# Gaps between on-chip buffers, and the last batch's router, norm and store in another order, in a one-core fp32r decoder layer

## The chip, the core and the metric

One NeuronCore of a Trainium2 chip runs the whole kernel. Its engines are TensorE (PE; PEld is its weight load), VectorE (DVE), ScalarE (ACT), GpSimd (POOL) and SyncE (SP), which here only issues DMAs. Each runs its own queue in the order in which the program was written, and they meet at semaphores. The metric is the device time of one launch in microseconds (us). Its operands lie in SBUF, 128 partitions wide. The address of a buffer below is the byte offset inside a partition.

## What is computed

A post-norm decoder layer over 16 batches of 256 tokens and 512 channels: causal attention with 16 query heads and 4 key/value heads, a WKV recurrence against a context, and a dense layer with a 16-expert low-rank adapter that a top-2 router weighs. Each ends in a residual sum and a layer norm.

```python
x = _layernorm(x + attention(x))            # H=16, HKV=4, HD=128, rotary, causal
x = _layernorm(x + wkv(w, u, k=x, v=ctx))   # scan over 256 tokens
# the last third, for every token of x:
h = silu(x @ rw1.T + rb1)
logits = (h @ rw2.T + rb2)[:, :16] + gates
topv, topi = top_k(logits, 2); sm = softmax(topv)
coeff = zeros_like(logits).at[rows, topi].set(sm)
base = x @ W.T + bias
delta = einsum('ner,eor->no', einsum('ni,eri->ner', x, A) * coeff[:, :, None], B)
x = _layernorm(x + base + delta)
```

## The kernel before

**Precision.** Every fp32 operand of a product is split in a high and a low half in the fp32r type (`Xh`, `Xl`, and so on), and `three` (lines 528 to 530) issues three matmuls for each product: high by high, high by low, low by high. Of the 10,500 matmuls in the trace 9,152 are of this kind. The others are transposes against the identity `Ident`, the router's second product (L722) and a warm-up (L738).

**Three stretches.** From slot 0 on, one attention head is taken up in each slot: projection, rotation, scores, softmax, product with V, output product, each some slots behind the other. A tail of the WKV recurrence for one batch runs through the same slots on DVE, ACT and POOL. The weights are staged in through `KVT`, `A2Z`, `E2Z` and `ED` and split on ACT (high) and DVE (low, `splits`, L1431) at slots that the table `SPLIT_AT` gives: the first half's pieces in the order `FIRST_ORDER`, DVE a slot behind ACT. Near the end the third part begins: `step(n, part)` for steps 0 to 19 with three parts each, written out by hand for each engine. The slots' table `PARTS_AT` interleaves the first of them with the last attention work; from about 1,315 us on they stand alone.

**A batch f in the steps.** In step f+1 PE transposes the rows (L667), in step f+2 it makes the low-rank and hidden product (320 columns), turns the hidden values (L713, part 1) and makes the logits (L722, part 2). DVE then picks the two best (L1408 to L1423), POOL makes the coefficients (L1116 to L1120) and weighs the low-rank values into `QB` (L1125). In step f+3 PE turns those (L701), makes the dense product in two halves of the rows (`dense(0)` in bank 5 in part 1, `dense(1)` in bank 6 in part 2, 12 matmuls of 512 columns each) and adds the adapter's product (6 matmuls for each half, `bank<-W,Qh`). In step f+4 DVE has added the residual (L1376), takes mean and variance (`norm_stats`, L1262 to L1267), POOL makes the scale and the shift (L1094 to L1098), ACT applies them (L947) and SP stores the 512 KB (L486). The last batch is f = 15, and `OUT[1]`, its output, lies in `XR`.

**Where the buffers lie.** They are allocated one behind the other. Modulo 128 bytes `W`, `smalls`, `tables` (cosine, sine, mask and identity), `Bo`, `XR`, `Xh`, `Xl`, `KHL`, `Vh`, `Vl`, `QB`, `SW`, `RC`, `KRC`, `Qh`, `Ql` and `S` start at 0; `PTh`, `PTl`, `OTh`, `OTl`, `RO`, `KVT`, `PS` and `ED` at 96, `A2Z` at 32, `E2Z` at 64, `QS` at 0.

Of the kernel before, what the change touches and what calls it, by code (L numbers as in the profile page):

```python
# [68 lines left out]
SPLIT_AT = [[-6, -6, -2, -2, -6, -6, 0, 1, 1, 2, 3, 4] + [h // 2 + 4 for h in range(HEADS)],  # L69
# [106 lines left out]
def decoder(nc, xt, xn, ctxt, wraw, small, bo, wf, wl, wb, fbias, trig_t, late_t, out):  # L176
# [4 lines left out]
    with ctx:  # L181
# [44 lines left out]
        both = lambda table: table[:, :].rearrange("p (a t) -> p a t", a=1).to_broadcast([P, 2, T])  # L226
        Q = [sb(f"Q{i}", [P, 2, T], fr) for i in "hl"]
# [3 lines left out]
        RL = sb("RL", [P, 2, TT])  # L231
        PT = [sb(f"PT{i}", [P, 4, P + T], fr) for i in "hl"]
# [181 lines left out]
        def _(sp):  # L414
# [55 lines left out]
            def step(n, part):  # L470
# [13 lines left out]
                if f is not None and part == 2:  # L484
                    sp.wait_ge(f_done, f + 1)
                    sp.dma_start(out[TAIL_BATCH[f], :, :].rearrange("(a p) c -> p a c", p=P), OUT[f % 2]).then_inc(f_out[f % 2], 16)  # L486
# [35 lines left out]
            for i in range(2):  # L522
                sp.wait_ge(f_out[i], 16 * BATCH // 2)

        @block.tensor
        def _(pe):
# [128 lines left out]
            def step(n, part):  # L655
# [13 lines left out]

                def dense(t):  # L670
# [32 lines left out]
                elif part == 1:  # L703
# [3 lines left out]
                    if f is not None:  # L707
# [6 lines left out]
                        last.then_inc(hid_turned, 1)  # L714
                else:
                    dense(1)
                    turn_x2(1)
                    f = stage_of(n, 2)
                    if f is not None:
                        pe.wait_ge(hid_copied, f + 1)  # L720
                        for a in range(TT):
                            last = nc.tensor.matmul(bank[4][:, T + a * EXP:T + (a + 1) * EXP], HST[:, a * P:(a + 1) * P], Rw2, start=True, stop=True)  # L722
                        last.then_inc(logits_done, 1)
# [18 lines left out]
        def _(act):  # L742
# [161 lines left out]
            def step(n, part):  # L904
# [26 lines left out]
                elif part == 1:  # L931
# [12 lines left out]
                    if f is not None:  # L944
                        act.wait_ge(f_shift, f + 1)
                        for t in range(TT):
                            last = nc.scalar.activation(OUT[f % 2][:, t, :], OUT[f % 2][:, t, :], ACT.Identity,  # L947
                                                        bias=NMF[:, f % 2, t:t + 1], scale=RSF[:, f % 2, t:t + 1])
                        last.then_inc(f_done, 1)
# [30 lines left out]
        def _(pool):  # L980
# [108 lines left out]
            def step(n, part):  # L1089
                f = stage_of(n, 4)  # L1090
                if f is not None and part == 0:
                    pool.wait_ge(f_ve, f + 1)
                    above(pool, f_done, f - 1)
                    gp.tensor_tensor(RSF[:, f % 2, :], VEF[:, f % 2, :], Mhalf[:, :], ALU.pow).then_inc(f_rs, 1)  # L1094
                    pool.wait_ge(f_rs, f + 1)
                    gp.tensor_tensor(NMF[:, f % 2, :], MVF[:, f % 2, :, 0], RSF[:, f % 2, :], ALU.mult).then_inc(f_rs2, 1)
                    pool.wait_ge(f_rs2, f + 1)
                    gp.tensor_scalar(NMF[:, f % 2, :], NMF[:, f % 2, :], -1.0, None, ALU.mult).then_inc(f_shift, 1)  # L1098
# [35 lines left out]
        def _(dve):  # L1134
# [125 lines left out]
            def norm_stats(tiles, par, stats, mv, ve, done):  # L1260
                for t in range(TT):
                    v.bn_stats(stats[:, par, t, :], tiles[:, t, :])  # L1262
                dve.drain()
                for t in range(TT):
                    v.bn_aggr(mv[:, par, t, :], stats[:, par, t, :])
                dve.drain()
                v.tensor_scalar(ve[:, par, :], mv[:, par, :, 1], EPS, None, ALU.add).then_inc(done, 1)  # L1267
# [93 lines left out]
            def step(n, part):  # L1361
# [16 lines left out]
                if part == 0:  # L1378
                    out_sum(4, 1)
                    f = stage_of(n, 4)  # L1380
                    if f is not None:
                        dve.wait_ge(f_sum, TT * f + TT)
                        above(dve, f_shift, f - 1)
                        norm_stats(OUT[f % 2], f % 2, STF, MVF, VEF, f_ve)
# [16 lines left out]
                else:  # L1401
# [24 lines left out]
                    out_sum(3, 0)  # L1426

# [74 lines left out]
```

## Time and profile before

| | us |
|---|---|
| median of 3 runs | 1603.1 |
| lowest, highest | 1602.74, 1606.97 |
| profiled execution, time | 1607.82 |
| profiled execution, span in the trace | 1606.0 |
| busy: PE / PEld / DVE / ACT / POOL | 1556.0 / 1413.4 / 1340.3 / 1115.5 / 1007.7 |
| mean granted TensorE clock, share of full speed | 0.991 |

The page's busy time of PE is the time in which at least one matmul is under way. Matmuls overlap, so the pace of a stream of them is read from the starts of neighbours in the timeline, not from the mean duration. The span is from the first to the last instruction; the profiled execution's time is 1.8 us longer.

### The profile page before, as it was taken

To read this page: it belongs to the slowest core of one execution; us is meant where nothing else is said; L and a number is where in the kernel's file an instruction comes from. 1 tells how busy PE (TensorE), PEld (TensorE's weight loads), DVE (VectorE), ACT (ScalarE), POOL (GpSimd) and SP (SyncE) were. 2 spreads that over 40 slices of the span, in tenths; PEclk is the share of its full clock that TensorE was granted. 3 is DMA by queue.
4 is the path that set the end of the run, shared out by engine and by line. 5 is a ranking of instruction groups with operands and counts; after the bars stand their busy time and mean duration, and the time that the engine had idled before them with its cause. 6 is when DMAs were issued, how large, how long until landed. Compare 5 with 4: busy or idle time off the path is not lost.

```text
span 1606.0 us, 32704 instructions
## 1 busy us (share of the span) xinstructions
PE 1556.0 (97%) x10500; PEld 1413.4 (88%) x10500; DVE 1340.3 (83%) x3434; ACT 1115.5 (69%) x2995; POOL 1007.7 (63%) x850
## 2 busy tenths in 40 slices
PE   8999999999999999999999999999999987989997
PEld 7899999999999999999999999999999976878785
DVE  6776688889888889898999889898989897877863
ACT  6777787877787778777877787878787865334332
POOL 2665586757675867676767666676667653635653
PEclk9999999999999999999999999999999999999999
DMA  9765344324442444244424442445144522121211
GB/s 298 256 225 201 112 150 137 116 73 142 150 137 55 152 146 136 60 152 151 139 60 152 151 139 60 132 146 164 44 126 148 178 70 79 53 93 66 80 66 53
DMA packets 81625, 202.62 MB, mean 126 GB/s; under 512 B 10416, under 2 KB 11056, under 8 KB 81456
## 3 DMA queue, kind: packets, MB, share of 16 engines
q1 hardware_dynamic: 81456, 200.53, 40.0%
q8 instruction: 86, 1.41, 0.4%
q14 instruction: 83, 0.68, 0.1%
HBM read 120.80 MB, written 37.75 MB: 99 GB/s over the span
## 4 chain that ended last, share of the span: by engine, by line
PE 84%; DVE 7%; issue 3%; POOL 2%; ACT 1%; DVEq 1%; DMA 1%; SPq 0%; ACTq 0%; POOLq 0%
PE bank L528 25%; PE bank L529 24%; PE bank L530 24%; PE bank L652 5%; PE bank L597 2%; PE bank L643 1%; PE bank L598 1%; PE bank L635 1%; DVE PS L1328 1%; DVE ED L1339 1%; PE bank L667 1%; DMA SW<-QB 1%; DVE SW L1392 0%; DVE RC L1170 0%; DVE OTl L1243 0%
## 5 line engine op out<-in xcount | busy, mean ns | idle before, releaser
L528 PE MATMUL bank<-Xh,W 128*128 128x256 f32 x1280 | 362.2, 283 | 5.8 <-DVE RC L1170 2.5
L529 PE MATMUL bank<-Xl,W 128*128 128x256 f32 x1280 | 360.5, 282 | 0.0
L530 PE MATMUL bank<-Xh,W 128*128 128x256 f32 x1280 | 360.4, 282 | 0.0
L1025 POOL TENSOR_TENSOR Ql<-RC,Qh 128x512 fp32r<-128x512 f32 x127 | 169.6, 1336 | 208.9 <-ACT Qh L744 208.7
L759 ACT ACTIVATE S<-S,NM 128x128 f32<-128x128 f32 (+1 forms) x512 | 228.2, 447 | 65.8 <-DVE NM L1155 65.2
L528 PEld LDWEIGHTS bank<-Xh,W 128*128 128x128 f32 x1280 | 241.3, 189 | 9.2 <-DVE RC L1170 5.1
L1013 POOL TENSOR_TENSOR SW<-SW,tables 128x512 f32<-128x512 f32 x128 | 170.8, 1334 | 124.6 <-DMA SW<-QB 124.5
L744 ACT ACTIVATE PTh<-bank 128x384 fp32r<-128x384 f32 x256 | 124.9, 488 | 173.1 <-PE bank L652 173.1
L529 PEld LDWEIGHTS bank<-Xl,W 128*128 128x128 f32 x1280 | 241.7, 189 | 0.0
L530 PEld LDWEIGHTS bank<-Xh,W 128*128 128x128 f32 x1280 | 241.6, 189 | 0.0
L744 ACT ACTIVATE S<-S,RL 128x128 f32<-128x128 f32 (+1 forms) x512 | 203.4, 448 | 31.7 <-DVE RL L1162 31.5
L528 PE MATMUL bank<-W,OTh 128*128 128x512 f32 x512 | 203.2, 397 | 4.9 <-DVE RO L1254 3.3
L529 PE MATMUL bank<-W,OTh 128*128 128x512 f32 x512 | 203.6, 398 | 0.0
L530 PE MATMUL bank<-W,OTl 128*128 128x512 f32 x512 | 203.1, 397 | 0.0
L1017 POOL TENSOR_TENSOR RC<-RC,SW 128x512 f32<-128x512 f32 x127 | 177.9, 1401 | 18.2
L528 PE MATMUL bank<-W,Xh 128*128 128x256 f32 (+2 forms) x512 | 166.4, 325 | 1.5 <-DVE RC L1170 1.4
L529 PE MATMUL bank<-W,Xh 128*128 128x256 f32 (+2 forms) x512 | 163.2, 319 | 0.0
L530 PE MATMUL bank<-W,Xl 128*128 128x256 f32 (+2 forms) x512 | 163.0, 318 | 0.0
L1170 DVE SCALAR_TENSOR_TENSOR RC<-bank,smalls,tables 128x256 f32<-128x256 f32 x256 | 119.6, 467 | 44.0 <-ACT QB L777 43.7
L1141 DVE TENSOR_TENSOR PTl<-bank,PTh 128x384 fp32r<-128x384 f32 x256 | 140.9, 550 | 2.2 <-ACT PTh L744 1.9
L1151 DVE TENSOR_TENSOR S<-bank,tables 128x128 f32<-128x128 f32 x256 | 72.5, 283 | 80.2 <-PE bank L530 79.7
L652 PE MATMUL bank<-tables,S 128*128 128x128 f32 x768 | 126.4, 273 | 1.5 <-DVE PTl L1141 1.4
(161 smaller groups left out, 4450.1 us busy)
## 6 DMA issues: line engine op xcount, KB each, us to landing
W<-kept SPq DMA_DIRECT2D x140, 512.0 KB, 4.5
SW<-QB SPq DMA_DIRECT2D x256, 128.0 KB, 2.3
kept<-W SPq DMA_DIRECT2D x40, 512.0 KB, 5.0
XR<-XR SPq DMA_DIRECT2D x64, 128.0 KB, 2.3
RO<-in_xn SPq DMA_DIRECT2D x16, 512.0 KB, 4.1
KVT<-in_ctxt SPq DMA_DIRECT2D x16, 512.0 KB, 4.2
mixed<-RO SPq DMA_DIRECT2D x16, 512.0 KB, 3.8
XR<-in_xt SPq DMA_DIRECT2D x15, 512.0 KB, 4.2
```

The costliest lines, as they stand in the source:

```text
L528: nc.tensor.matmul(dst, lhs[0], rhs[0], start=first, stop=False)
L529: nc.tensor.matmul(dst, lhs[0], rhs[1], start=False, stop=False)
L530: return nc.tensor.matmul(dst, lhs[1], rhs[0], start=False, stop=last)
L652: last = nc.tensor.transpose(pt_ps[:, k * P:(k + 1) * P], S[:, g % 2, k * P:(k + 1) * P], Ident[:, :])
L744: return nc.scalar.activation(dst, src, ACT.Copy, **kw)
L759: last = nc.scalar.activation(S[:, i, c], S[:, i, c], ACT.Exp, bias=NM[:, i, t:t + 1], scale=-1.0, accum_out=L[:, i, t:t + 1])
L1013: gp.tensor_tensor(SW[:, :, :], SW[:, :, :], both(Sin), ALU.mult).then_inc(q_sin, 1)
L1017: gp.tensor_tensor(RC[:, i % 2, :, :], RC[:, i % 2, :, :], SW[:, :, :], ALU.add).then_inc(q_summed, 1)
L1025: gp.tensor_tensor(Q[1][:, :, :], RC[:, i % 2, :, :], Q[0][:, :, :], ALU.subtract).then_inc(q_lo, 1)
L1141: v.tensor_tensor(PT[1][:, g % 4, :], pt_ps[:, 0:P + T], PT[0][:, g % 4, :], ALU.subtract).then_inc(pt_lo, 1)
L1151: v.tensor_tensor(S[:, i, 0:P], s_ps[:, P:T], Mask[:, 0:P], ALU.add).then_inc(masked, 1)
L1170: v.scalar_tensor_tensor(out=RC[:, g // 2 % 2, g % 2, :], in0=proj_ps("Q", g, 0), scalar=Bq[:, SEQ[g // HEADS][0], h:h + 1], in1=Cos[:, :] ...
```

## The change

It has five parts. (1) Four buffers named gap0 to gap3 that nothing reads or writes, 64, 64, 64 and 32 bytes wide, are allocated in front of `Xh`, of `KHL`, of `Qh` and of `PTh`. Modulo 128 `Xh`, `Xl`, `Qh`, `Ql`, `S`, `PTh`, `PTl`, `OTh`, `OTl`, `RO`, `KVT`, `PS` and `ED` then start at 64, `A2Z` and `QS` at 0 and 96, `E2Z` at 32, and the others stay at 0. (2) The weight piece of the first half's fifth query head is split a slot later, together with the sixth's. (3) For the last batch PE makes the logits right behind the turned hidden values, in part 1 of step 17, ahead of `dense(1)` of batch 14. (4) For the last batch DVE takes the statistics of the first 128 rows before it adds the residual of the second 128, and POOL and ACT work on each half by itself. (5) The last batch is stored in two DMAs of 256 KB.

```diff
-SPLIT_AT = [[-6, -6, -2, -2, -6, -6, 0, 1, 1, 2, 3, 4] + [h // 2 + 4 for h in range(HEADS)],
+SPLIT_AT = [[-6, -6, -2, -2, -6, -6, 0, 1, 2, 2, 3, 4] + [h // 2 + 4 for h in range(HEADS)],
...
+        def gap(i, n):
+            sb(f"gap{i}", [P, n // 4])
         XR = sb("XR", [P, KC, T])
+        gap(0, 64)
         X = [sb(f"X{i}", [P, 2, KC, T], fr) for i in "hl"]
+        gap(1, 64)
         KHL = sb("KHL", [P, 2, JL, 2, T], fr)
...
+        gap(2, 64)
         Q = [sb(f"Q{i}", [P, 2, T], fr) for i in "hl"]
         S = sb("S", [P, 2, P + T])
...
+        gap(3, 32)
         PT = [sb(f"PT{i}", [P, 4, P + T], fr) for i in "hl"]
...
-                    sp.wait_ge(f_done, f + 1)
-                    sp.dma_start(out[TAIL_BATCH[f], :, :].rearrange("(a p) c -> p a c", p=P), OUT[f % 2]).then_inc(f_out[f % 2], 16)
+                    rows = out[TAIL_BATCH[f], :, :].rearrange("(a p) c -> p a c", p=P)
+                    if f < LAST:
+                        sp.wait_ge(f_done, f + 1)
+                        sp.dma_start(rows, OUT[f % 2]).then_inc(f_out[f % 2], 16)
+                    else:
+                        for t in range(TT):
+                            sp.wait_ge(f_done, f + t + 1)
+                            sp.dma_start(rows[:, t, :], OUT[f % 2][:, t, :]).then_inc(f_out[f % 2], 16)
...
+                def logits():
+                    f = stage_of(n, 2)
+                    if f is not None:
+                        pe.wait_ge(hid_copied, f + 1)
+                        for a in range(TT):
+                            last = nc.tensor.matmul(bank[4][:, T + a * EXP:T + (a + 1) * EXP], HST[:, a * P:(a + 1) * P], Rw2, start=True, stop=True)
+                        last.then_inc(logits_done, 1)
...
                         last.then_inc(hid_turned, 1)
+                        if f == LAST:
+                            logits()
                 else:
                     dense(1)
                     turn_x2(1)
-                    f = stage_of(n, 2)
-                    if f is not None:
...
+                    if stage_of(n, 2) != LAST:
+                        logits()
...
-                        act.wait_ge(f_shift, f + 1)
                         for t in range(TT):
+                            act.wait_ge(f_shift, f + 1 + t * (f == LAST))
                             last = nc.scalar.activation(OUT[f % 2][:, t, :], OUT[f % 2][:, t, :], ACT.Identity,
                                                         bias=NMF[:, f % 2, t:t + 1], scale=RSF[:, f % 2, t:t + 1])
-                        last.then_inc(f_done, 1)
+                            if f == LAST or t == TT - 1:
+                                last.then_inc(f_done, 1)
...
+                    for k, those in enumerate((slice(0, 1), slice(1, 2)) if f == LAST else (slice(0, TT),)):
+                        pool.wait_ge(f_ve, f + k + 1)
+                        gp.tensor_tensor(RSF[:, f % 2, those], VEF[:, f % 2, those], Mhalf[:, those], ALU.pow).then_inc(f_rs, 1)
...
-                        norm_stats(OUT[f % 2], f % 2, STF, MVF, VEF, f_ve)
+                        norm_stats(OUT[f % 2], f % 2, STF, MVF, VEF, f_ve, range(f == LAST, TT))
...
                     out_sum(3, 0)
+                    if stage_of(n, 3) == LAST:
+                        dve.wait_ge(f_sum, TT * LAST + 1)
+                        dve.wait_ge(f_shift, LAST - 1)
+                        norm_stats(OUT[LAST % 2], LAST % 2, STF, MVF, VEF, f_ve, range(1))
```

Line numbers of the changed kernel are some lines higher: L528 to L530 become L546 to L548, L713 becomes L739, L722 L693, L1376 L1403, L1431 L1462.

**PE, step 17**, where the logits of the last batch stand. Before:

```order
L530 MATMUL bank5<-W,Xl 128x512
L713 MATMUL bank4<-tables,SW 64x128 x2
L528 MATMUL bank6<-W,Xh 128x512
L529 MATMUL bank6<-W,Xh 128x512
...
L530 MATMUL bank6<-W,Xl 128x512
L722 MATMUL bank4<-smalls,SW 128x16 x2
L528 MATMUL bank5<-W,Qh 128x512
```

And in the changed kernel:

```order
L548 MATMUL bank5<-W,Xl 128x512
L739 MATMUL bank4<-tables,SW 64x128 x2
L693 MATMUL bank4<-smalls,SW 128x16 x2
L546 MATMUL bank6<-W,Xh 128x512
L547 MATMUL bank6<-W,Xh 128x512
...
L548 MATMUL bank6<-W,Xl 128x512
L546 MATMUL bank5<-W,Qh 128x512
```

The two logits matmuls have moved past the 12 matmuls of `dense(1)` of batch 14.

**DVE, the last rows of the program**, behind the low half of the last adapter operand (`Ql`). Before:

```order
L1398 TENSOR_TENSOR Ql<-bank1,Qh 128x512
L1376 TENSOR_TENSOR XR<-bank5,KRC 128x512
L1376 TENSOR_TENSOR XR<-bank6,S 128x512
L1262 BN_STATS STF<-XR 128x6 x2
L1265 BN_AGGR MVF<-STF 128x2 x2
L1267 TENSOR_SCALAR VEF<-MVF 128x2
```

And in the changed kernel:

```order
L1425 TENSOR_TENSOR Ql<-bank1,Qh 128x512
L1403 TENSOR_TENSOR XR<-bank5,KRC 128x512
L1288 BN_STATS STF<-XR 128x6
L1291 BN_AGGR MVF<-STF 128x2
L1294 TENSOR_SCALAR VEF<-MVF 128x1
L1403 TENSOR_TENSOR XR<-bank6,S 128x512
L1288 BN_STATS STF<-XR 128x6
L1291 BN_AGGR MVF<-STF 128x2
L1294 TENSOR_SCALAR VEF<-MVF 128x1
```

The first half's statistics now stand between the two residual sums.

**DVE, slots 2 to 4 at the start**, the low halves of the weight pieces (`W<-E2Z,W`, `W<-ED,W`) among the first heads' work. Before:

```order
L1431 TENSOR_TENSOR W<-E2Z,W 128x512
L1431 TENSOR_TENSOR W<-ED,W 128x512
L1170 SCALAR_TENSOR_TENSOR RC<-bank0,smalls,tables 128x256
L1216 TENSOR_TENSOR Vl<-bank1,Vh 128x256
L1202 TENSOR_TENSOR KHL<-KRC,KHL 128x2x256
L1183 TENSOR_TENSOR RC<-RC,SW 128x512
L1186 TENSOR_TENSOR Ql<-RC,Qh 128x512
L1431 TENSOR_TENSOR W<-ED,W 128x512
L1170 SCALAR_TENSOR_TENSOR RC<-bank1,smalls,tables 128x256
```

And in the changed kernel:

```order
L1462 TENSOR_TENSOR W<-E2Z,W 128x512
L1196 SCALAR_TENSOR_TENSOR RC<-bank0,smalls,tables 128x256
L1242 TENSOR_TENSOR Vl<-bank1,Vh 128x256
L1228 TENSOR_TENSOR KHL<-KRC,KHL 128x2x256
L1209 TENSOR_TENSOR RC<-RC,SW 128x512
L1212 TENSOR_TENSOR Ql<-RC,Qh 128x512
L1462 TENSOR_TENSOR W<-ED,W 128x512 x2
L1196 SCALAR_TENSOR_TENSOR RC<-bank1,smalls,tables 128x256
```

One low half has moved behind the first heads' `Ql`; its high half on ACT has moved in the same way, from ahead of the third head's `QB` to just ahead of the `KHL` copy.

## Rows read from the trace of the kernel before

**Rows 1.** Busy time by stretch: start:end, its length, PE's busy time, granted clock, DMA share, GB/s

```profile
100.00:1290.00 1190.00, 1188.65 (x8384) 1.00 0.42 130
...
1354.00:1364.00 10.00, 7.20 (x38) 1.00 0.16 52
...
1481.00:1491.00 10.00, 8.25 (x44) 1.00 0.01 2
...
1587.00:1592.00 5.00, 5.00 (x19) 0.66 0.26 100
```

**Rows 2.** Timeline of PE: start, duration, what; ends of three even runs of matmuls

```profile
502.59 0.39 PE L528 MATMUL bank<-W,OTh 128*128 128x512 f32 x1
...
503.75 0.40 PE L530 MATMUL bank<-W,OTl 128*128 128x512 f32 x1
...
505.73 0.29 PE L528 MATMUL bank<-Xh,W 128*128 128x256 f32 x1
...
508.10 0.28 PE L530 MATMUL bank<-Xh,W 128*128 128x256 f32 x1
...
1594.30 0.40 PE L528 MATMUL bank<-W,Qh 128*128 128x512 f32 x1
...
1596.86 0.40 PE L530 MATMUL bank<-W,Ql 128*128 128x512 f32 x1
```

**Rows 3.** Groups of PE instructions by line: transposes, busy us, mean ns, idle before

```profile
L643 PE MATMUL bank<-tables,E2Z 128*128 128x128 f32 x128 | 19.8, 278 | 3.7 <-DVE RO L1350 3.7
L635 PE MATMUL bank<-tables,RO 128*128 128x128 f32 x128 | 19.5, 275 | 3.0 <-DVE RO L1350 1.6 <-ACT KVT L744 1.4
```

**Rows 4.** Two lines' POOL instructions: count, duration ns min/median/max, first and last start

```profile
L1062 POOL TENSOR_TENSOR E2Z<-PS,KVT x32: 1085/1287/1539, 234.4 to 1504.9; 128x512 f32<-128x512 f32 x32
...
L1025 POOL TENSOR_TENSOR Ql<-RC,Qh x127: 1267/1292/2222, 31.8 to 1314.6; 128x512 fp32r<-128x512 f32 x127
```

**Rows 5.** Timeline of all engines, steps 17 and 18: the last batch's router

```profile
1578.04 0.38 ACT L744 ACTIVATE SW<-bank 64x256 f32<-64x256 f32 x1 [1.53 <-PE bank L713]
...
1580.71 0.61 PE L722 MATMUL bank<-smalls,SW 64*128 64x16 f32 x4
...
1581.36 0.19 DVE L1408 TENSOR_TENSOR S<-bank,smalls 128x32 f32<-128x32 f32 x1 [3.71 <-PE bank L722]
...
1583.91 0.40 PE L530 MATMUL bank<-W,Ql 128*128 128x512 f32 x1
...
1586.68 0.66 PE L701 MATMUL bank<-tables,QB 128*128 128x128 f32 x4 [2.38 <-POOL QB L1125]
...
1587.10 0.48 PE L528 MATMUL bank<-W,Xh 128*128 128x512 f32 x1
```

**Rows 6.** Timeline of all engines, the last batch's residual, norm and store

```profile
1597.29 0.69 DVE L1376 TENSOR_TENSOR XR<-bank,S 128x512 f32<-128x512 f32 x1 [0.71 <-PE bank L530]
1598.02 1.29 DVE L1262 BATCH_NORM_STATS2 STF<-XR 128x6 f32<-128x512 f32 x2
...
1599.95 0.71 POOL L1094 TENSOR_TENSOR RSF<-VEF,Mhalf 128x2 f32<-128x2 f32 x1 [11.62 <-DVE VEF L1267]
...
1601.29 1.52 ACT L947 ACTIVATE XR<-XR,NMF,RSF 128x512 f32<-128x512 f32 x2 [11.41 <-POOL NMF L1098]
1602.84 0.37 SPq L486 DMA_DIRECT2D out_x<-XR  x1
```

**Rows 7.** DMA issues by line: count, KB each, median us to landing

```profile
out_x<-XR SPq DMA_DIRECT2D x2, 512.0 KB, 2.7
...
SW<-QB SPq DMA_DIRECT2D x256, 128.0 KB, 2.3
```

**Rows 8.** Timeline of the start, slots 2 to 5

```profile
23.12 0.69 DVE L1431 TENSOR_TENSOR W<-ED,W 128x512 fp32r<-128x512 f32 x1
...
28.42 0.47 ACT L777 ACTIVATE QB<-bank,smalls 128x256 f32<-128x256 f32 x1 [2.05 <-DMA SW<-QB]
...
29.46 0.39 PE L528 MATMUL bank<-Xh,W 128*128 128x256 f32 x1 [1.43 <-DVE RC L1170]
```

More of the change, by code:

```diff
@@ L406, in run @@
                     step(n, part)
+        LAST = BATCH - 1
         def stage_of(n, lag):
@@ L522, in _ @@
             for i in range(2):
-                sp.wait_ge(f_out[i], 16 * BATCH // 2)
+                sp.wait_ge(f_out[i], 16 * (BATCH // 2 + (i == LAST % 2)))
         @block.tensor
@@ L717, in step @@
                     turn_x2(1)
-                    f = stage_of(n, 2)
-                    if f is not None:
[L720 to L723, printed above, removed]
+                    if stage_of(n, 2) != LAST:
+                        logits()
                     f = stage_of(n, 3)
@@ L1091, in step @@
                 if f is not None and part == 0:
-                    pool.wait_ge(f_ve, f + 1)
                     above(pool, f_done, f - 1)
[L1094 to L1098, printed above, removed]
+                    for k, those in enumerate((slice(0, 1), slice(1, 2)) if f == LAST else (slice(0, TT),)):
+                        pool.wait_ge(f_ve, f + k + 1)
+                        gp.tensor_tensor(RSF[:, f % 2, those], VEF[:, f % 2, those], Mhalf[:, those], ALU.pow).then_inc(f_rs, 1)
+                        pool.wait_ge(f_rs, f + k + 1)
+                        gp.tensor_tensor(NMF[:, f % 2, those], MVF[:, f % 2, those, 0], RSF[:, f % 2, those], ALU.mult).then_inc(f_rs2, 1)
+                        pool.wait_ge(f_rs2, f + k + 1)
+                        gp.tensor_scalar(NMF[:, f % 2, those], NMF[:, f % 2, those], -1.0, None, ALU.mult).then_inc(f_shift, 1)
                 f = stage_of(n, 2)
@@ L1258, in odd, with norm_stats @@
                 tail(n, 0)
-            def norm_stats(tiles, par, stats, mv, ve, done):
-                for t in range(TT):
+            def norm_stats(tiles, par, stats, mv, ve, done, which=range(TT)):
+                for t in which:
                     v.bn_stats(stats[:, par, t, :], tiles[:, t, :])
                 dve.drain()
-                for t in range(TT):
+                for t in which:
                     v.bn_aggr(mv[:, par, t, :], stats[:, par, t, :])
                 dve.drain()
-                v.tensor_scalar(ve[:, par, :], mv[:, par, :, 1], EPS, None, ALU.add).then_inc(done, 1)
+                those = slice(which.start, which.stop)
+                v.tensor_scalar(ve[:, par, those], mv[:, par, those, 1], EPS, None, ALU.add).then_inc(done, 1)
             def norm_shift(par, mv, rs, nm):
```

## Prediction

> **What bounds the kernel now.** I read the busy time by stretch first. From 100 to 1,290 us PE is busy for 1,188.65 of 1,190 us at a granted clock of 1.00, the higher of the two levels, 2.4 GHz [rows 1]. In that stretch nothing but the pace of PE's own stream counts: what is gained on DVE, ACT or POOL comes to nothing there. So the change has two places where it can act: the pace of the matmuls, which the gaps might touch, and the ends of the program, where PE waits and where the last batch's norm and store hang behind it.
>
> **The gaps, PE.** After them the moving and the stationary operand of nearly all products lie 64 bytes apart modulo 128 (`Xh` 64 and `W` 0, `Qh` 64 and `KHL` 0, `PTh` 64 and `Vh` 0, `OTh` 64 and `W` 0). Before, they are 0 apart (`Xh`/`W`, `Qh`/`W`) or 32 apart (`OTh`/`W`). The timeline gives the paces [rows 2]: 20 matmuls of 256 columns, 0 apart, from 505.73 to 508.10, 118.5 ns each; 5 of 512 columns, 32 apart, from 502.59 to 503.75, 232.0 ns; 11 of 512 columns, 0 apart, from 1594.30 to 1596.86, 232.7 ns. So 0 or 32 apart makes 0.7 ns of 232, or 0.3%. The nearest to 64 are the transposes of `E2Z`, whose blocks lie 68 to 80 bytes from the identity's: 278 ns in the mean beside 275 ns for those of `RO`, 32 apart [rows 3]. No row has an fp32r pair 64 apart. I take 0 for it, since neither the one step shown nor the nearest neighbour moves the pace. The bounds are 0.3% of the 1,189 us either way, 3.6 us, and a rival below takes what lies beyond.
>
> The trace has both of PE's streams, moving data and the next weights, under way at once at this pace, whatever lies where. The Trainium skill (SBUF — State Buffer, Who interferes with whom) gives PE two independent read ports and says that PE and ACT never wait on anyone; by that rule this term is exactly 0, and no row here contradicts it, but none is at 64. The same notes (TensorE: Matmul & The Clock Gate, Back-to-back issue gap) give N/2.4 + 2.5 ns for isolated matmuls, 109.2 and 215.8 ns for 256 and 512 columns. If the rest of the 118.5 and 232.7 ns were a conflict that the gaps end, an estimate by that page over some 6,000 and 2,500 matmuls would be 56 + 42 = 98 us off, about 1,500 us. I do not use it in the sum.
>
> **The gaps, POOL and DVE.** The duration of a GpSimd sum does depend on something of this kind: the same line L1062 takes 1,085 ns at least and 1,287 ns in the median, and its two halves differ in nothing but their addresses (`PS` 0 or 8 bytes past `KVT` modulo 128) [rows 4]. `Ql<-RC,Qh`, now 0 apart and then 64, takes 1,292 ns in the median [rows 4]. 127 of those, anything from 26 us of POOL's time off to as much on, all of it beside a PE that does not wait [rows 1]. Worth 0; that cover is gone only where PE waits for `Ql` in the first 50 us, three waits, so 0.2 us each: 0.6 us either way.
>
> **The logits ahead of `dense(1)`.** Now PE turns the hidden values, ACT copies them from 1578.04 to 1578.42, and PE comes to the logits only at 1580.71, behind 12 matmuls. DVE begins at 1581.36, and POOL's `QB` lets PE go on at 1586.68, after 2.38 us of idleness; PE's last matmul before that started at 1583.91 [rows 5]. In the new order PE waits for ACT's copy: logits at 1578.50 instead of 1580.71, so DVE, and all that follows on DVE, ACT and POOL, 2.2 us earlier, and `QB` lets PE go at 1584.5. ACT has its norm of batch 13 between the copy and the router's exponential, 1.5 us by the like of it [rows 6], over at about 1579.8, when the exponential's input is due. What is queued behind the new wait on PE is `dense(1)` and the adapter of batch 14: 12 matmuls that started behind the turn now start behind the logits, PE idles about 0.5 us, and its last matmul starts at about 1584.5 instead of 1583.91. DVE's residual of batch 14 waits for that, 0.6 us later, and the last batch's `dense` products, which need the bank, do not: they start later still. Now both PE and `QB` are due at 1584.5, so PE turns `QB` at about 1584.75, **1.9 us earlier**. What is late next is PE itself.
>
> **The clock.** PE's granted clock reads 0.66 from 1587 to 1592, a stretch in which PE never stops, right after the 2.38 us of idleness [rows 1, 5]. The 24 matmuls of both `dense` halves took 1587.10 to 1594.30, 7.20 us, where 24 at 232.7 ns are 5.58: **1.6 us** lost. Around 1481 to 1491 PE is idle for 1.75 us in sum and the clock stays at 1.00 [rows 1]. With 0.5 us of idleness left I expect no fall. Against it: from 1354 to 1364, with 2.8 us idle, it did not fall either [rows 1], so whether it falls is not settled by the gap alone, and the runs near the median may not all have had it.
>
> **The norm and the store by halves.** Take PE's last matmul start, 1596.86, as T [rows 2]. Now the second residual starts at T + 0.43, both statistics at T + 1.16, POOL at T + 3.09, ACT at T + 4.43, the store at T + 5.98, and the span ends 3.16 us later [rows 6]. The first half's residual stands 6 matmuls earlier, at T - 0.97, done at T - 0.28. Its statistics take 1.93 us less one of the two passes and one aggregation, about 1.2 us, so DVE is free at T + 0.95: the second residual is 0.5 us late, and the second statistics, shorter by 0.7, are done at T + 2.9, about 0.15 us earlier than now. POOL does the first half's three steps meanwhile (1.34 us). So ACT scales the second half at T + 4.3 for half of 1.52 us, and the last store is issued at T + 5.1 instead of T + 5.98: 0.9 us. The store then carries 256 KB. By the rows a 512 KB store lands after 2.7 us and a 128 KB copy after 2.3 [rows 7]; the last one's 3.16 us less 0.2 to 0.9, I take 0.5. The other half has landed by then. **1.4 us** in sum. The Trainium skill (SBUF — State Buffer, The DMA setup-cost knee) has about 2 us fixed and the bytes at 436 GB/s behind them: 0.6 us less for half the bytes, so 1.5 us by that page.
>
> **The start.** DVE has 0.69 us [rows 8] of splitting less before the first `Ql` and as much more behind it; on ACT one high half, 0.53 us, slips ahead of the `KHL` copy. Ahead of it nothing is won: the work that follows waited for PE. Behind it `Ql` is 0.5 us and the next head's `RC` 1.1 us later. PE's next wait, 1.43 us at 29.46, ends with `RC`, which waits for `QB`, which waits 2.05 us for a DMA [rows 8]. If that DMA is held up by its backlog, the delay is swallowed; if it starts 0.5 us later, all behind it is 0.5 us later. **0.3 us** lost, between 0 and 1.1.
>
> **The sum.** 1.9 + 1.6 + 1.4 - 0.3 = 4.6 us, with 0 for the gaps. Against the profiled execution, 1607.8 - 4.6 = 1603.2. That execution is 4.7 us slower than the median, and I do not know which waits or clock falls make this; I take the same 4.6 us off the median: **1598.5 us**. Without the clock term it is 1600.1; with PE's pace 0.3% better 1594.9, and 0.3% worse 1602.1.
>
> **Rivals.**
> *The gaps speed up the fp32r matmuls.* For it: the pace above the columns alone. From 256 to 512 columns it grows by 114.2 ns, so some part is not columns; POOL's line shows that addresses can matter on this chip. Against it: 0 and 32 apart are alike. Each ns is 9.2 us on 9,152 matmuls: 1 ns gives 1589.3, 5 ns 1552.5.
> *The gaps slow them down.* Same place, the other sign: if 64 apart costs, the 4.6 us are eaten at 0.5 ns for each of the 9,152, and at 1 ns the kernel stands at 1607.7, slower than before. Against it: the same two paces.
> *The ends give back less.* The clock falls anyway, at another place, and the start costs 1.1 us: 4.6 - 1.6 - 0.8 = 2.2, so 1600.9. For it: the fast runs, of which I have no trace.
>
> **Chances.** Forecast 0.55, own range 1594.9 to 1602.1; gaps faster 0.20; gaps slower 0.07; less at the ends 0.18. A measurement of this kernel tells 0.3%, 4.8 us, from no change: the bound is 1598.3 and the forecast lies on it. So half of its 0.55 goes to faster, with 0.20 from the gaps: 0.48. Same has the other half and 0.18: 0.45. Slower 0.07. The range takes the forecast's and the lesser gain, and of the faster gaps the part up to 1 ns: 1589 to 1603.
>
> **What would show it.** Right: matmul starts 118.5 and 232 ns apart as before; the last batch's logits 0.5 us behind the turn of its hidden values; PE idle under 0.7 us ahead of the last turn of `QB`; granted clock 1.00 behind it; two stores, the last issued 5.1 us behind PE's last start. Wrong: another pace in the middle stretch, where 1 ns outweighs all the rest twice over; a clock fall in the last 20 us; a first PE wait beyond 50 us.

## The result, and the profile after

| us | before | after | ratio (95%) |
|---|---|---|---|
| median, 4 runs each, beside one another | 1604.7 (1602.7 to 1607.0) | 1588.5 (1586.0 to 1590.6) | 0.9898 (0.9875 to 0.9921) |
| profiled execution: time, span | 1607.8, 1606.0 | 1587.5, 1585.7 | |

Faster by 16 us, 1.0%. The forecast was 1598.5, its range 1589 to 1603: the time lies half a microsecond below the range. In a later round (`after_again`, below) the changed kernel had 1588.8 beside 1608.5, ratio 0.9876 (0.9861 to 0.9891).

The busy time by stretch, which answers to [rows 1] (start:end, length, PE's busy time, granted clock, DMA share, GB/s):

```profile
100.00:1290.00 1190.00, 1180.79 (x8449) 1.00 0.42 130
...
1570.00:1575.00 5.00, 5.00 (x26) 1.00 0.01 3
```

PE starts 65 matmuls more in the same 1,190 us (8,449 beside 8,384) although it is busy for 7.9 us less. The two lines of each pair below are the first and the last start of an even run, at the place of [rows 2]: 24 projections of 256 columns and 6 output products of 512 in the changed kernel.

```profile
500.33 0.28 PE L546 MATMUL bank<-Xh,W 128*128 128x256 f32 x1
...
502.96 0.28 PE L548 MATMUL bank<-Xh,W 128*128 128x256 f32 x1
503.07 0.39 PE L546 MATMUL bank<-W,OTh 128*128 128x512 f32 x1
...
504.22 0.40 PE L548 MATMUL bank<-W,OTl 128*128 128x512 f32 x1
```

23 steps in 2.63 us are 114.3 ns each, where [rows 2] have 118.5; 5 steps in 1.15 us are 230 ns, where they have 232. And PE now waits in the middle. Waits of PE between 60 and 1,290 us (what waits, for what, us in total, times, longest), where the kernel before has one line, `RC`, 0.6 us in 2:

```profile
PE bank L546 <- DVE RC L1196: 5.9, 13, 0.8
PE bank L661 <- DVE RO L1377: 1.6, 4, 0.5
PE bank L546 <- DVE OTl L1269: 1.4, 1, 1.4
PE bank L615 <- POOL Ql L1050: 0.2, 1, 0.2
```

Since both kernels issue the same 10,500 matmuls in nearly the same order, the starts can be subtracted one by one. A step between neighbours is counted as a wait where in either kernel it is over 90 ns longer than usual for its width, and as pace otherwise (us):

| up to matmul | start before | start after | earlier by | pace | waits |
|---|---|---|---|---|---|
| 9,000 | 1287.3 | 1274.5 | 12.75 | +20.3 | -7.5 |
| 10,000 | 1495.5 | 1481.9 | 13.6 | +21.1 | -7.5 |
| the last | 1596.9 | 1578.4 | 18.5 | +22.1 | -3.6 |
| span's end | 1606.0 | 1585.7 | 20.3 | | |

So up to matmul 10,000 PE's pace gave 21.1 us and new waits took 7.5 back; behind it the end gave 4.9, and what follows PE's last start 1.9. The 20.3 are 14.3 from `Xh` and `Xl` moving, 4 from output products (`OTh`), 1.1 from `PTl`. A second trace of the same kernel (`after_again`) has the same pace by matmul 9,000, +20.6, but waits of -9.9: the waits differ by 2 us between executions, the pace hardly.

The end, timeline of all engines, answers to [rows 5, 6]:

```profile
1563.26 0.38 ACT L768 ACTIVATE SW<-bank 64x256 f32<-64x256 f32 x1 [1.49 <-PE bank L739]
1563.69 0.61 PE L693 MATMUL bank<-smalls,SW 64*128 64x16 f32 x4 [0.47 <-ACT SW L768]
...
1569.67 0.39 PE L548 MATMUL bank<-W,Ql 128*128 128x512 f32 x1
...
1569.90 0.60 PE L727 MATMUL bank<-tables,QB 128*128 128x128 f32 x4
...
1578.40 0.40 PE L548 MATMUL bank<-W,Ql 128*128 128x512 f32 x1
...
1579.19 0.15 DVE L1294 TENSOR_SCALAR VEF<-MVF 128x1 f32<-128x1 f32 x1
1579.26 0.68 DVE L1403 TENSOR_TENSOR XR<-bank,S 128x512 f32<-128x512 f32 x1
...
1580.69 0.81 ACT L971 ACTIVATE XR<-XR,NMF,RSF 128x512 f32<-128x512 f32 x1 [4.98 <-POOL NMF L1124]
...
1581.53 2.08 SPq L504 DMA_DIRECT2D out_x<-XR  x2
...
1582.43 0.81 ACT L971 ACTIVATE XR<-XR,NMF,RSF 128x512 f32<-128x512 f32 x1 [0.93 <-POOL NMF L1124]
```

PE waits 0.47 us for the hidden values and not at all for `QB`; the store goes out in two halves.

### The profile page after: what moved, and what is told of

Read it like the earlier page. It is cut to its first block, busy times and chain, and to the rows that moved or that the text cites. A ratio compares the mean times of both kernels' runs of the same rounds, so it can differ in the third digit from the quotient of the medians.

```text
span 1585.7 us, 32712 instructions
## 1 busy us (share of the span) xinstructions
PE 1533.6 (97%) x10500; PEld 1395.1 (88%) x10500; DVE 1337.7 (84%) x3435; ACT 1114.7 (70%) x2995; POOL 1007.2 (64%) x853
## 4 chain that ended last, share of the span: by engine, by line
PE 68%; DVE 14%; issue 6%; ACT 5%; POOL 5%; DMA 1%; DVEq 1%; SPq 0%; ACTq 0%; POOLq 0%
PE bank L546 20%; PE bank L548 20%; PE bank L547 19%; PE bank L670 4%; DVE PS L1325 2%; PE bank L615 1%; DMA SW<-QB 1%; DVE PS L1355 1%; DVE RC L1196 1%; PE bank L653 1%; PE bank L661 1%; ACT Xh L768 1%; DVE PTl L1167 1%; DVE OTl L1269 1%; POOL SW L1038 1%
## 5 line engine op out<-in xcount | busy, mean ns | idle before, releaser
L546 PE MATMUL bank<-Xh,W 128*128 128x256 f32 x1280 | 357.5, 279 | 8.1 <-DVE RC L1196 5.5
L548 PE MATMUL bank<-Xh,W 128*128 128x256 f32 x1280 | 356.0, 278 | 0.0
L547 PE MATMUL bank<-Xl,W 128*128 128x256 f32 x1280 | 355.7, 278 | 0.0
L1050 POOL TENSOR_TENSOR Ql<-RC,Qh 128x512 fp32r<-128x512 f32 x127 | 170.4, 1342 | 195.8 <-ACT Qh L768 195.5
L783 ACT ACTIVATE S<-S,NM 128x128 f32<-128x128 f32 (+1 forms) x512 | 228.2, 448 | 67.9 <-DVE NM L1181 67.5
L546 PEld LDWEIGHTS bank<-Xh,W 128*128 128x128 f32 x1280 | 241.4, 189 | 11.3 <-DVE RC L1196 6.6
L548 PEld LDWEIGHTS bank<-Xh,W 128*128 128x128 f32 x1280 | 241.0, 188 | 0.0
L546 PE MATMUL bank<-W,OTh 128*128 128x512 f32 x512 | 201.5, 394 | 5.0 <-DVE RO L1280 3.3
L548 PE MATMUL bank<-W,OTl 128*128 128x512 f32 x512 | 203.0, 396 | 0.0
L546 PE MATMUL bank<-W,Xh 128*128 128x256 f32 (+2 forms) x512 | 165.5, 323 | 2.9 <-DVE RC L1196 2.9
L548 PE MATMUL bank<-W,Xl 128*128 128x256 f32 (+2 forms) x512 | 161.5, 315 | 0.0
```

The source lines that it names most:

```text
L546: nc.tensor.matmul(dst, lhs[0], rhs[0], start=first, stop=False)
L547: nc.tensor.matmul(dst, lhs[0], rhs[1], start=False, stop=False)
L548: return nc.tensor.matmul(dst, lhs[1], rhs[0], start=False, stop=last)
L783: last = nc.scalar.activation(S[:, i, c], S[:, i, c], ACT.Exp, bias=NM[:, i, t:t + 1], scale=-1.0, accum_out=L[:, i, t:t + 1])
L1050: gp.tensor_tensor(Q[1][:, :, :], RC[:, i % 2, :, :], Q[0][:, :, :], ALU.subtract).then_inc(q_lo, 1)
```

## The experiments

**1. The parts apart.** `gaps_only` is before with the four gaps, `ends_only` the changed kernel without them and with the old slot in `SPLIT_AT`.

> The kernel before with the four gaps and nothing else. Theory A (an fp32r matmul starts sooner behind its neighbour when moving and stationary operand lie 64 bytes apart modulo 128): 11 to 15 us off, ratio 0.991 to 0.993, about 13.6 us less at the last matmul, since the trace of the changed kernel gains 13.6 us by its 10,000th matmul, ahead of the edits at the end; Xh and W products of 256 columns start 114.9 ns apart instead of 118.7. Rival B (the ends, or the split moved by a slot, made most of the gain): within 4 us of before, ratio 0.998 to 1.002.

> The changed kernel without the gaps and with the old slot for the fifth query head's weight piece: only the last batch's logits, norm and store are changed. Theory A: 4.9 us off as predicted, between 4 and 7, ratio 0.9955 to 0.9975. Rival B: 12 us or more off.

| | median | before beside it | ratio (95%) | pace, waits to matmul 9,000 |
|---|---|---|---|---|
| `gaps_only` | 1593.8 | 1609.0 | 0.9909 (0.9896 to 0.9923) | +20.2, -8.2 |
| `ends_only` | 1602.8 | 1609.0 | 0.9958 (0.9944 to 0.9972) | none |

The gaps alone give 15 us and the ends 6. Their sum, 21 us, is more than the 16 of the result and near the 19.7 of `after_again`. Rival B is out.

**2. Distance or place.** `all_shifted` has one gap of 64 bytes in front of `W`; nothing moves against anything else.

```diff
+        gap(9, 64)
         W = sb("W", [P, NP, 2, PW], fr)
```

> The kernel before with one 64-byte gap ahead of W, so that W and every buffer behind it move by 64 bytes and no two of them move against each other. Theory A (it is the distance between the two operands): no change, ratio 0.998 to 1.002, 118.7 ns as before. Rival C (it is where a moving operand itself lies, 64 instead of 0): as much as the gaps alone, ratio 0.991 to 0.993.

1606.8 beside 1609.0, ratio 0.9989 (0.9980 to 0.9999); the pace to matmul 9,000 differs by 0.25 us. The same 24 projections:

```profile
505.51 0.28 PE L532 MATMUL bank<-Xh,W 128*128 128x256 f32 x1
...
508.23 0.28 PE L534 MATMUL bank<-Xh,W 128*128 128x256 f32 x1
```

118.3 ns, as before. So it is how the buffers lie against one another, not where they all lie. The medians of the 12 steps of a query projection, over 191 groups, are 119 118 118 117 120 119 115 117 122 120 119 118 ns in both; in the changed kernel they are 114 and 113. Medians over all groups hide two kinds there: right behind the product with V (`PTh` by `Vh`) all 112 groups free of waits run at 113 ns from their first step on (1,360 ns for 12), but those behind the scores (`KHL`) begin, in the median, with 118 121 116 115 ns and fall to 114 only then.

**3. PE alone, first program.** 60 matmuls in a row, one buffer for each distance.

> Another program: 60 matmuls in a row on 128 partitions with nothing between them, for each distance of the moving operand (Ma 0 bytes modulo 128, Mb 16, and so on to Mh 112) from the stationary one (Sa 0, Se 64), for 256 and 512 columns of fp32r, twice over; then 128 columns of fp32r and of fp32 (F) at 0 and 64. It computes nothing of the reference. Theory A: for 256 columns about 118.7 ns apart at distance 0 and 114.9 at 64, for 512 columns 232.5 and 229, and Se with Me (both at 64) as Sa with Ma. Rival C: Se with Me as Sa with Me. Rival D (the pace depends on the other engines' traffic, not on PE's own two reads): all distances alike.

Paces behind the first ten matmuls, from the second sweep (the first agrees to 0.1 ns but for its first stream, at a lower clock, and one of 512): at 0, 16, 32, 48, 64, 80, 96, 112 bytes, 256 columns 120.0, 118.7, 116.7, 119.2, 117.8, 119.2, 120.0, 117.1 and 512 columns 226.7, 233.3, 233.3, 233.3, 228.9, 230.0, 233.3, 236.7 ns; 128 columns 111.7 throughout. `Se` with `Me` is 118.7 and 232.4, neither as `Sa` with `Ma` nor as `Sa` with `Me`. So addresses matter with no other engine at work, against rival D, but neither theory A nor rival C had the values.

**4. Which gap.** `x_only` has the first two gaps, `rest_only` the last two.

> The kernel before with the gaps ahead of Xh and of KHL only: X moves by 64 bytes, all behind it by 128. Theory A: 3.9 ns on 3,520 projections with X moving, 2.1 on 960 with W moving and some ns on 352 of 512 columns make 16 to 17 us of pace; with the new waits on DVE 8 to 13 us less, ratio 0.992 to 0.995.

> The kernel before with the gaps ahead of Qh and of PTh only: Q, PT, OT and all behind them move, X and W stay. Theory A: 3.5 ns on 1,536 output products is 5.4 us, less 9 ns on 192 and more 2 ns on 512 of the probabilities' about even: 3 to 7 us off, ratio 0.9955 to 0.998. If the gaps ahead of X make all of the gain: ratio 0.999 to 1.001.

`x_only`: 1596.4 beside 1606.2, 0.9941 (0.9927 to 0.9955), pace +12.2, waits -4.3. `rest_only`: 1604.6, 0.9991 (0.9983 to 1.0000), pace +0.7, waits -0.4: less than expected. Together they make 20.3, so 7.4 us belong to neither. The steps show where. Of the 112 query projections behind the product with V, 67 run at 117 to 118 ns to their end with `X` alone (1,412 ns for 12) and 45 take 1,387; before, all take about 1,417, with all gaps 1,360. Behind the scores they begin, in the median, with 121 122 116 115 ns and then fall to 114. `Xh` lies as far from `W` in both kernels, so this distance is not all that counts. That the matmuls ahead, whose operands the other gaps move, leave something behind fits these steps; it is not shown apart from them.

**5. PE alone, the kernel's patterns.** Groups of `three`, the kernel's strides, one operand read from 0 to 112 bytes on.

> Another program, computing nothing of the reference: PE alone, with the kernel's own groups of three matmuls, their accumulation and their strides, on buffers that all begin at 0 modulo 128, and one operand read from 0, 16, 32 ... 112 bytes behind its buffer's start. Seven patterns, 56 streams of 60 to 96 matmuls: query projection (X moving 256), value projection (W moving 256), output (OT stationary, W moving 512), dense (X stationary, W moving 512), low (the same with 320), scores, probabilities by V. The uniform streams before gave 120.0 and 117.8 ns at distance 0 and 64 for 256 columns but 226.7 and 228.9 for 512, so the distance alone does not order the paces. Theory A (PE's two reads by themselves, in the kernel's pattern): query projection 118.7 ns at 0 and 114.9 at 64, value projection 118.3 and 116.3, output 232 at 96 and 229 at 64, each within 0.5 ns of what the kernels' traces show. Rival D (the other engines' traffic is needed): the same two streams differ by less than 1 ns, or as in the uniform streams.

Query projections 117.8 ns at all distances but 96 (118.6); value projections 119.2 at 0 and 113.3 at 64; output and dense products, with the same addresses, agree within 0.3 ns and go from 230.0 (48) to 235.6 (16). Theory A missed all three patterns: 117.8 ns for 114.9 in the query projections at 64; 119.2 and 113.3 for 118.3 and 116.3 in the value projections, the right sign at three times the size; 233.3 (96) and 231.9 (64) for 232 and 229 in the output products.

> Another program, computing nothing of the reference, PE alone. Query projections by themselves were 117.8 ns apart whatever the distance, while value projections went from 119.2 at 0 to 113.3 at 64, and in the changed kernel both are seen. Theory E (the pace of a matmul depends on the addresses and on what state the stream before it left): 60 query projections at distance 64 run at 113 to 114 ns behind 12 value projections and at 117.8 behind an idle engine; at distance 0 they stay at 118 to 120 behind either. Then 8 slots of one position in the kernel's own order (scores, probabilities by V, projections, output, transposes), 286 matmuls with nothing of the other engines, in 11 sets of distances (X, Q, PT, OT, S). Theory A in this wider form: before's set to the changed kernel's set, the slots get 60 to 70 ns for each projection of 12 shorter, as in the kernels (1421 to 1360 ns), about 2% in sum, x_only between them, rest_only within 0.3% of before. Rival D (other engines' traffic is needed): the four sets within 0.3%.

It had 280 matmuls for each set. Query projections at 64 behind value projections: 117.1 ns, not 113. The four sets took 39.61, 39.58, 39.49 and 39.61 us. Theory E and the wider theory A failed, and D seemed to hold. What I had overlooked: the buffers of these programs lay other than the kernel's modulo 256. In the kernel `Xh` minus `W` was 128 before and is 192 now; in these programs, at "64" modulo 128 `Xh` in my query stream was at 64 modulo 256, and `W` minus `Xh` in my value stream at 192; `Xl` lay another 128 bytes off, since `Xh` was 8,320 bytes long.

**6. Modulo 256.** Buffers all alike modulo 2,048, 16 offsets, and the 8 slots in the kernels' own distances.

> Another program, computing nothing of the reference, PE alone. The slots of the last one did not show the kernels' difference (1405 to 1420 ns for 12 projections in both sets), but its buffers lay other than the kernels' modulo 256. Theory F (the distance that counts is moving minus stationary address modulo 256, and 192 is the fast one): before 128, the changed kernel 192 for Xh against W; value projections in the small programs at 64 were W minus X = 192, and fast; query projections there at 64, and not. So 60 query projections at 192 take 113.3 ns each and 117 to 119 elsewhere, value projections 113.3 at 64 and slower elsewhere, and 192 + 256, + 512 and + 1,024 are as 192. The 8 slots in the kernels' own distances modulo 2,048: 12 projections 1,421 ns by before's and 1,360 by the changed kernel's, 1.5 to 2% in sum. If Theory F is wrong the two sets differ by less than 0.3%, as in the last program, and the other engines' traffic is needed (Rival D).

Windows over single streams: query projections at 128 and 192, value projections with `X` at 64 and 192; query projections at 704 and 448; then the 8 slots by before, the changed kernel, `x_only`, `rest_only`:

```profile
101.90:109.40 7.50, 7.32 (x60) 1.00 0.01 2
132.50:139.90 7.40, 7.09 (x60) 1.00 0.00 0
193.30:200.80 7.50, 7.09 (x60) 1.00 0.00 0
254.40:262.00 7.60, 7.34 (x60) 1.00 0.01 2
757.10:764.70 7.60, 7.33 (x60) 1.00 0.00 0
749.80:757.20 7.40, 7.09 (x60) 1.00 0.01 2
803.10:843.50 40.40, 40.07 (x280) 1.00 0.01 1
843.50:883.20 39.70, 39.40 (x280) 1.00 0.00 1
883.20:923.00 39.80, 39.62 (x280) 1.00 0.00 1
923.00:963.30 40.30, 40.02 (x280) 1.00 0.00 1
```

7.09 us are 113.3 ns a matmul once the stream runs, 7.3 are 117.8 to 118.7. Query projections are fast at 192 (and at 112), value projections with `X` at 64, which is `W` minus `X` at 192. The slots are 1.7% (by the changed kernel's distances), 1.1% (`x_only`) and 0.1% (`rest_only`) shorter than by before's; the kernels' pace to matmul 9,000 is 20.3, 12.2 and 0.7 us better of 1,287: 1.6, 0.9 and 0.1%. PE's own reads suffice for a difference of this size, and rival D is out. Not all of theory F holds: 448 is fast, but 704 and 1,216, also 192 modulo 256, ran at 117.8 ns from an idle engine.

The same in the kernel: `other_64` has `gap(0, 192)` and `gap(1, 192)`, so `Xh` minus `W` is 64 modulo 256.

> The changed kernel with the first two gaps 192 bytes wide instead of 64: Xh still lies 64 bytes from W modulo 128, but at 64 instead of 192 modulo 256, and everything behind KHL stays where it was modulo 256. Theory A as first stated (modulo 128): as the changed kernel, ratio 0.988 to 0.991. Theory F (modulo 256): query projections about 117.8 ns apart instead of 114.8, 3 ns on 3,520, 10 us, value projections 3 ns less on 960, 3 us back: ratio 0.993 to 0.995.

```profile
502.43 0.28 PE L546 MATMUL bank<-Xh,W 128*128 128x256 f32 x1
...
505.15 0.28 PE L548 MATMUL bank<-Xh,W 128*128 128x256 f32 x1
```

118.3 ns. Behind the product with V all query projections are at 117 to 118 ns a step (1,413 for 12). Value projections are of two kinds, nearly in turn: 29 groups at 113 to 114 ns and 29 at 118. The single stream had 113.3 for this distance only; and the changed kernel has 21 of 56 at 113 and `x_only` 30 of 57 at `W` minus `X` = 64, where the stream had 117.8. So for value projections the distance modulo 256 does not tell the pace. 1593.1 beside 1608.7, 0.9907 (0.9894 to 0.9921): pace +11.4, waits -4.1, so 8.9 us of pace are lost against the changed kernel, of which 3.4 come back as waits that go too; the ratio lies between the forecasts of theories A and F. Everything behind `KHL` has also moved by 256 bytes here, which theory F takes for nothing.

**7. What limits next.** DVE's two scans stand ahead of the rotation `RC` for which PE waits. Timeline of DVE in the changed kernel:

```profile
461.25 1.74 DVE L1348 TENSOR_TENSOR_SCAN QS<-A2Z,E2Z 128x514 f32<-128x514 f32 x1
462.92 2.24 DVE L1355 TENSOR_TENSOR_SCAN PS<-A2Z,E2Z 128x514 f32<-128x514 f32 x1
465.08 0.13 DVE L1188 RECIPROCAL RL<-L 128x2 f32<-128x2 f32 x1
465.14 0.46 DVE L1196 SCALAR_TENSOR_TENSOR RC<-bank,smalls,tables 128x256 f32<-128x256 f32 x1
```

```diff
-PS_AT = [(10, 1), (12, 0)]
+PS_AT = [(11, 0), (12, 0)]
```

> The changed kernel with one DVE scan (PS, first half, 2.2 us) a slot later, so that it does not stand right behind the scan of QS in front of the rotation RC for which PE now waits 0.3 to 0.9 us in 13 slots (5.9 us in sum). If these waits cost what they show: 3 to 6 us less than the changed kernel, ratio to before 0.986 to 0.988. Rival (DVE's work is only moved, and PE waits a slot later): as the changed kernel, 0.990.

1593.1 beside 1606.8, 0.9913 (0.9897 to 0.9929): no gain, as the rival has it. PE now waits 8.1 us for `RC` in 17 places.

> The changed kernel with DVE's four scans of each recurrence (QS 1.74 us, PS 2.24 us) replaced by plain sums of the same operands, some 0.6 us each: DVE has about 5.5 us less in each of 16 tails, and the second third of the layer is not computed rightly. Theory G (behind the faster PE, DVE is the next bound, and the new waits are its): PE's waits between 60 and 1,290 us fall from 12.6 us to under 5, and the time is 6 to 10 us less than the changed kernel's, ratio to before 0.984 to 0.986. Rival (the waits come from elsewhere): ratio as the changed kernel's, 0.989.

> The kernel before with the same cheap scans, again not the reference's second third. Theory G: PE waited only 3.2 us in the middle stretch, so at most that comes back, 0 to 3 us, ratio 0.998 to 1.000, against 6 to 10 us in the changed kernel. Rival: as much as there.

In both kernels the cheap sums leave out the recurrence. The cut for `PS`; `QS` has the same:

```diff
-v.tensor_tensor_scan(in_row(PS, h), in_row(A2Z, h), in_row(E2Z, h), 0.0, ALU.mult, ALU.add).then_inc(ps_done, 1)
+v.tensor_tensor(in_row(PS, h), in_row(A2Z, h), in_row(E2Z, h), ALU.add).then_inc(ps_done, 1)
```

1576.9 and 1599.8 beside 1608.5: 0.9797 (0.9783 to 0.9810) and 0.9945 (0.9931 to 0.9959). PE's waits in the changed kernel, with cheap scans:

```profile
PE bank L661 <- DVE RO L1377: 2.0, 5, 0.5
...
PE bank L546 <- DVE RC L1196: 0.5, 2, 0.3
```

The waits for `RC` are gone but for 0.5 us, and 11.9 us in all beside the changed kernel's 1588.8, more than either expectation. But before gains 8.7 too, against my expectation: 2.7 by matmul 9,000 and most of the rest behind it. By matmul 9,000 the cheap scans give 6.6 us beside the changed kernel's first trace and 8.6 beside its second, so 3.9 to 5.9 of them are owed to the faster PE (3 by the medians of the whole). The cheap scans take away more than the order of DVE's work, so the last pair changes only the order.

```diff
+                if tail_of(n, 11) is None:
                     cosines(n)
...
                         if h == 0:
+                            cosines(n + 1)
                             dve.wait_ge(z_done, 2 * tau + 2)
```

> The changed kernel with DVE's rotation RC of the next head put between the two scans QS and PS (1.7 and 2.2 us) instead of behind both, in the 32 slots where they stand together; nothing is left out and no load changes. PE waits 5.9 us in 13 places for just this RC. Theory G: those waits go, PE's waits between 60 and 1,290 us fall from 12.6 to about 7 us, ratio to before 0.984 to 0.987 where the changed kernel has 0.988 to 0.990. Rival (PE catches up with another DVE result a few instructions on, as with the scan put later): 0.988 to 0.991.

**1582.8** beside 1607.2, 0.9847 (0.9833 to 0.9860). The changed kernel had 0.9898 and 0.9876, so this is 5 to 8 us faster, and the intervals do not touch. Pace +20.9, waits -2.4 instead of -7.5 and -9.9. DVE:

```profile
460.45 1.74 DVE L1349 TENSOR_TENSOR_SCAN QS<-A2Z,E2Z 128x514 f32<-128x514 f32 x1
462.12 0.45 DVE L1196 SCALAR_TENSOR_TENSOR RC<-bank,smalls,tables 128x256 f32<-128x256 f32 x1
462.49 1.87 DVE L1357 TENSOR_TENSOR_SCAN PS<-A2Z,E2Z 128x514 f32<-128x514 f32 x1
```

**8. Can the small program choose distances?** `gap(2, 192)` and `gap(3, 160)`, in the changed kernel and with the rotation first.

> The changed kernel with the third gap 192 bytes wide instead of 64 and the fourth 160 instead of 32: Q and S 128 bytes further, at 192 instead of 64 from W modulo 256, all behind PT at 256 further and so the same modulo 256. In the program of PE alone 8 slots took 38.93 us with this distance and 39.13 with the changed kernel's, 0.20 us over 32 positions: 6.4 us less pace. Theory F with G: PE's pace 5 to 7 us better by the starts, of which DVE lets through a part, 2 to 5 us, ratio to before 0.986 to 0.989. If the small program does not foretell a kernel: 0.989 or more.

> The same with the third gap 192 and the fourth 160 bytes wide. Its pace in the trace was 2.3 us worse than the changed kernel's by the 9,000th matmul and its waits 1.5 us less, so the same as the run before it within 2 us: ratio 0.984 to 0.988.

`q_further`: 1588.2, 0.9876 (0.9860 to 0.9891), as the changed kernel beside it; its pace is 2.3 us worse, not 6.4 better. `rotation_first_q`: 1585.3, 0.9866 (0.9851 to 0.9881). Of the 113 query projections behind the product with V in `q_further`, 54 now take about 1,413 ns, where all took 1,360. But this was not a clean trial of the small program. Its set for `q_further` left `PT` and `OT` at 448 and the transposed rows at 1,344 modulo 2,048, and in the kernel `PT` and `OT` lie at 704 and `S` at 1,472. That 256 bytes more can change a pace, the single streams had shown: 448 is fast and 704 is not. Whether the small program gets 0.5% right with the kernel's true distances was not tried.

**9. The start and the measure.**

> The changed kernel with the fifth query head's weight piece split in its old slot. By my step the start is 0.3 us better, between 0 and 1.1; the traces of the first 80 us say the move gained about 1 us, so up to 1 us slower. Ratio to before 0.989 to 0.991 either way.

> The changed kernel itself, beside the other three on their chip: ratio 0.988 to 0.992 as measured before.

`after_old_start`: 1588.4 beside 1606.8, 0.9886 (0.9871 to 0.9901): no difference that can be told.

## Why the prediction was wrong, step by step

**The gaps, PE: 0 with bounds of 3.6 us. This step failed.** Measured 20 to 22 us of pace. Three things were wrong in it. The bounds came from "neither the one step shown nor the nearest neighbour moves the pace": one difference between two distances, taken for a flat curve, where the small program (`micro_256`) has 113.3 to 120.0 ns between 16 offsets. The neighbour was no neighbour: transposes of 128 columns take 109 ns a step in every trace, their mean durations 278 and 276 now beside 278 and 275 [rows 3]; nor does the stream of 128 fp32r columns move. And distances were taken modulo 128, where the streams at 0 and 128 bytes (120.0 and 118.7 ns), and at 64 and 192 (117.8 and 113.3), differ. The mean of 118.5 ns hid a pattern of 115 to 122 that a look at single steps in the trace of before would have shown.

By the rule of the Trainium skill (SBUF — State Buffer, Who interferes with whom), two independent read ports for PE, which never waits on anyone, this term would be exactly 0. The small programs, with PE alone, do not bear it out for PE's own two reads: 7.09 or 7.3 us for the same 60 matmuls, by their addresses.

**Rival: the gaps speed up fp32r matmuls**, chance 0.20, was right in its mechanism: addresses set part of the pace above the columns. The 22 us are 2.4 ns in the mean by its 9.2 us per ns; the range took only the first ns.

**"What is gained on DVE ... comes to nothing there" [rows 1]** was not quite so for before, and wrong behind a faster PE. With cheap scans before gains 3.1 us between 100 and 1,287 us, mostly in eleven places where a projection starts 0.18 to 0.45 us sooner, though the view of its waits shows only 0.6 us. With DVE's order changed behind the faster PE 5.7 to 7.8 us come out of the same stretch. The rival lacked this too: 7.5 to 9.9 of its 20 us went into waits, most of them for `RC`.

**The gaps, POOL and DVE: 0.** Right. POOL is busy for 1007.2 us (1007.7 before), and `Ql<-RC,Qh` means 1,342 ns (1,336), though its operands moved by 64:

```profile
L1050 POOL TENSOR_TENSOR Ql<-RC,Qh 128x512 fp32r<-128x512 f32 x127 | 170.4, 1342 | 195.8 <-ACT Qh L768 195.5
```

**The logits, 1.9 us.** Right. PE waits 0.47 us for them (0.5 said), and PE itself is what is late next. Matmuls 10,120 to 10,460 hold both the old wait for `QB` and the new one for the logits: 67.5 to 67.9 us in the six kernels with the old end, 65.5 to 65.9 in the ten traces with the new one: 2.1 us.

**The clock, 1.6 us.** The size is right, the occurrence is not certain. The last 39 matmuls take 10.2 us in before and in `gaps_only` and 10.0 in `before_cheap_scans`, 8.5 to 8.6 in those ten, but also in `all_shifted`, `x_only` and `rest_only`, which have the old end. Windows around PE's last wait, in before, `gaps_only` and `all_shifted`:

```profile
1584.90:1590.90 6.00, 4.22 (x15) 0.75 0.03 9
```

```profile
1568.80:1574.80 6.00, 4.12 (x13) 0.72 0.01 3
```

```profile
1582.50:1588.50 6.00, 3.62 (x18) 1.00 0.01 3
```

So behind the same wait the clock fell in some executions and not in others: "Whether it falls is not settled by the gap alone" was right, and the median of before probably holds only a part of the 1.6 us. The same executions differ by another 1.1 us that I had not seen: between matmul 10,000 and 10,120 before and `gaps_only` take 23.46 us and the others 22.3 to 22.4 (the late scan 23.1, `before_cheap_scans` 23.0). In before PE waits 1.08 us there for `QB`, in the changed kernel 0.21:

```profile
1498.72 0.66 PE L727 MATMUL bank<-tables,QB 128*128 128x128 f32 x4 [0.21 <-POOL QB L1151]
```

2.1, 1.7 and 1.1 make the 4.9 us of the end. The 1.7 and the 1.1 are absent in other traces with the old end, so they are not sure to be in a median of before.

**Norm and store by halves, 1.4 us.** 1.9: from PE's last start to the span's end 9.2 us became 7.3. ACT scales the second half at T + 4.03 (4.3 said). The last store is issued at T + 4.87 (5.1 said), and the end is 2.4 us behind it instead of 3.16 (2.66 said):

```profile
1583.27 0.34 SPq L504 DMA_DIRECT2D out_x<-XR  x1
```

`ends_only` gives 6.3 us by its medians where these three steps sum to 4.9: right in kind.

**The start, 0.3 us lost.** Open. By its trace `after_old_start` stands 3.4 us later than the changed kernel at matmul 500. But two executions of the changed kernel itself differ by 1.5 us there (79.6 and 81.1 us; before 80.6), and the ratios agree: 0.9886 (0.9871 to 0.9901) with the old start, 0.9898 and 0.9876 with the new one.

## What to carry to other kernels

Where PE is bound by its own stream of fp32r matmuls, look at the single steps between starts, by what stands ahead of each group: if steps of one shape differ and repeat from group to group, the distance between moving and stationary operand is worth a few tens of bytes of padding. The distance modulo 256 did not tell every pace here, so try it on the kernel itself, and if a small program is to choose, give it all the kernel's distances. Then ask what the faster stream will wait for: here new waits took back 7.5 to 9.9 of 20 us, and putting one short rotation between two scans instead of behind them gave 5 to 8 us more.

## What the runs showed of the hardware that I had not expected

- PE alone, at a granted clock of 1.00, runs a stream of 256-column fp32r matmuls at 113.3 to 120.0 ns and one of 512 at 226.7 to 236.7, by the operands' addresses; 128 columns stay at 111.7. Moving every buffer by 64 bytes changes nothing (ratio 0.9989, pace 0.25 us of 1,287).
- The pace is a repeating pattern (before: 115, 118, 122, 120, 119 ns, then again), and with the same distances modulo 256 in one kernel the same pair ran at 113 or at 117 to 121: in `x_only`, `other_64` and `q_further` fast and slow groups of one product stand beside one another. Whether that comes from the stream ahead or from wider differences of address was not told apart.
- Not settled: why 192 and 448 bytes are fast and 704 and 1,216 not in a stream that starts from an idle engine, while in the changed kernel, at 1,216, all groups behind the product with V run at 113. What in the memory makes the pattern wasn't looked into.
- The same wait of PE at the same place was followed by a granted clock of 0.75 in the mean of 6 us in some executions and of 1.00 in others.
